# One meeting between phases, pads written by ScalarE, ternary weights prepared later, and products that nothing reads

## The reference

```
x = x + L0_xattn(layernorm(x), ctx)     # phase xatt0: q, wq, o, wp quantised to int8 steps, 16 heads of 16
x = x + L0_ffn(layernorm(x))            # phases gqa (causal attention) and moe0 (8 experts, top 2)
x = x + L1_xattn(layernorm(x), ctx, mask)   # phase mask_bit, first part
x = x + L1_ffn(layernorm(x))                # phase mask_bit, second part
x = x + L2_xattn(layernorm(x), ctx)     # phase xatt2
x = x + L2_ffn(layernorm(x))            # phase arrow
x = x + L3_xattn(layernorm(x), ctx)     # phases qkv3 and attend3
x = x + L3_ffn(layernorm(x))            # phase moe3

   # L1_xattn: one head of width 256, masked
scores = where(mask, x @ ctx.T / 16, -1e30);  out = softmax(scores) @ ctx
   # L1_ffn: three ternary weight matrices of 256 x 1024
weight_quant(w): s = 1 / max(mean(|w|), 1e-5);  clip(round(w * s), -1, 1) / s
gate, up = bit_linear(x, w_gate), bit_linear(x, w_up)
out = bit_linear(subln(up * relu(gate) ** 2), w_down)      # bit_linear also rounds x to 8-bit steps
   # L3_xattn: q, k rounded to 8-bit steps per row, v per column
q, k, v = qdq(x @ Wq / 4), qdq(ctx @ Wk), qdq(ctx @ Wv)
```

## Time and profile before

| | us |
|---|---|
| median of 3 runs | 3013.79 |
| lowest, highest | 3013.21, 3014.51 |
| the profiled execution | 3008.75 |
| its span | 3007.0 |

### The profile page before, as it was taken

How to read it: one execution, slowest core, us unless ns; L and a number is a source line. 1 busy time by engine, 2 the same in 40 slices (tenths; PEclk the granted TensorE clock), 3 DMA queues, 4 the chain that set the end, 5 groups by cost and what they waited for, 6 DMA issues and landing times. The chain is left out here.

```text
span 3007.0 us, 51047 instructions
## 1 busy us (share of the span) xinstructions
PE 2461.1 (82%) x19764; PEld 1665.5 (55%) x19788; DVE 2106.1 (70%) x4548; ACT 1633.5 (54%) x2824; POOL 543.0 (18%) x410
## 2 busy tenths in 40 slices
PE   6969999987999575897976577777777777779999
PEld 4736676764666343674655444444444444446666
DVE  7857878764352586775757799999999999942231
ACT  4534545543233364443434588888888888832222
POOL 2224333321221233221320400000000000012121
PEclk9989999998999677999998799999999999989999
DMA  3120000002000211101012300000000000000000
GB/s 136 39 78 6 11 8 18 6 4 77 21 22 11 91 36 67 33 26 43 29 43 89 133 9 9 15 9 9 14 17 9 9 15 9 3 27 21 11 11 11
DMA packets 58942, 92.83 MB, mean 31 GB/s; under 512 B 5440, under 2 KB 54608, under 8 KB 57680
## 3 DMA queue, kind: packets, MB, share of 16 engines
q1 hardware_dynamic: 58704, 89.57, 8.9%
HBM read 66.48 MB, written 23.07 MB: 30 GB/s over the span
## 5 line engine op out<-in xcount | busy, mean ns | idle before, releaser
L2595 ACT ACTIVATE attend_ex<-psum,attend_mx,queries_step 128x1024 uint16<-128x1024 f32 x512 | 618.0, 1207 | 122.0 <-DVE attend_mx L2626 122.0
L2697 PEld LDWEIGHTS psum<-ident_b,attend_ex 128*128 128x128 bf16 x4096 | 250.3, 100 | 398.9 <-issue 397.8
L2697 PE MATMUL psum<-ident_b,attend_ex 128*128 128x128 bf16 x4096 | 326.4, 225 | 157.0 <-DVE attend_pw L2630 125.9
L2685 PE MATMUL psum<-keys_turned,queries_ahead 96*128 96x512 bf16 x1024 | 320.1, 396 | 79.5 <-ACT attend_ex L2595 74.6
L1460 PE MATMUL psum<-arena,moe_tokT 128*128 128x512 f32 (+2 forms) x896 | 362.0, 549 | 3.3 <-DVE moe_h L1347 3.3
L2619 DVE TENSOR_REDUCE attend_mx<-psum 128x1 f32<-128x512 f32 x512 | 329.8, 686 | 26.1 <-PE psum L2685 7.8
L2615 DVE TENSOR_REDUCE attend_mx<-psum 128x1 f32<-128x1024 f32 x256 | 311.2, 1216 | 7.2 <-PE psum L2685 7.1
L1347 DVE TENSOR_TENSOR moe_h<-moe_sg,psum 128x512 f32<-128x512 f32 (+1 forms) x112 | 69.9, 625 | 267.0 <-PE psum L1460 257.5
L1460 PEld LDWEIGHTS psum<-arena,moe_tokT 128*128 128x128 f32 x896 | 166.5, 192 | 139.4 <-issue 120.9
L1194 ACT ACTIVATE moe_sg<-psum 128x512 f32<-128x512 f32 (+1 forms) x112 | 61.4, 548 | 287.1 <-PE psum L1460 282.8
L1130 POOL IOTA moe_index<- 128x8 f32 x2 | 0.3, 142 | 1007.0 <-POOLq L67 1007.0
(11 more groups left out here) (457 smaller groups left out, 4800.8 us busy)
## 6 DMA issues: line engine op xcount, KB each, us to landing
residual<-stored_rows SPq DMA_DIRECT2D x48, 128.0 KB, 1.7
queries_turned<-queries_rows SPq DMA_DIRECT2D x16, 384.0 KB, 3.1
queries_ahead<-queries_turned SPq DMA_DIRECT2D x16, 384.0 KB, 3.3
arena<-in_moe SPq DMA_DIRECT2D x1, 5704.0 KB, 16.4
arena<-in_gqa SPq DMA_DIRECT2D x1, 5440.0 KB, 18.4
arena<-in_moe SPq DMA_DIRECT2D x1, 4360.0 KB, 13.3
xatt_ct<-in_ctx_T SPq DMA_DIRECT2D x32, 128.0 KB, 2.3
residual<-stored_rows SPq DMA_DIRECT2D x16, 256.0 KB, 2.2
```

Of the source, the lines that this page charges most:

```text
L2595: nc.scalar.activation(ex[:, u % 4], S[:, u % 3], ACT.Exp, bias=mx[:, t % 2, h, 4:5], scale=steps[:, 0, t, h:h + 1], accum_out=sums[:, t % ...
L2685: last = nc.tensor.matmul(S[:, u % 3, b * 512:(b + 1) * 512], qt[:, t % 2, h * P:(h + 1) * P], KT[:, c:c + 4, h // 2], start=True, stop=True)
L2697: last = nc.tensor.transpose(TP[:, c], counts[u % 4][:, c * P:(c + 1) * P], k["ident_b"][:])
```

## The change

Six edits in one.

1. `end_phase` is gone. Between phases only the meeting at the end of the block is left. The semaphores of the last two phases are held, and the spent ones are cleared by POOL inside the next phase (`clear_spent`, at one place of each phase's POOL program). At the end of the program `end_program` has the two meetings and the clears.
2. The pads of xatt0 and xatt2 are written by ACT as 11 strided activations (Copy of `neg_half` broadcast, times a factor; together 2304 elements a partition), ahead of its other work; `Qp` in qkv3 as one activation of 128 x 3072.
3. gqa's causal mask is made behind the second `rstd`, and PE waits for it only before the first scores.
4. The ternary preparation in moe0 comes later: sums at steps 3 to 5, total at 6, steps, clamps and rounds at 6 and 7, casts at 7 to 9.
5. mask_bit: the mask is the first DMA, and x_norm of the first pair comes ahead of the wait for it.
6. `keep_busy`: products of `ident_b` with itself (128 x 512, bf16) that nothing reads, on PE: in mask_bit 12 at step 0 and 7 at each of steps 1 to 7, between `down` and `turn_b`; in qkv3 5 at the start of each of steps 1 to 16, from step 3 behind a wait for `qT`. 141 products in all.

```diff
-def end_phase(nc, sems):
-
-    numbers = sorted(s.num for s in sems.values())
+def semaphores(nc, k, phase, names):
+    if len(k["held"]) == 2:
+        k["held"].pop(0)[0].close()
+    stack = ExitStack()
+    sems = {n: stack.enter_context(nc.semaphore(phase + n)) for n in names.split()}
+    k["held"].append((stack, sorted(v.num for v in sems.values())))
+    return sems
+
+def clear_numbers(nc, numbers):
+    start = numbers[0]
+    for n, following in zip(numbers, numbers[1:] + [-1]):
+        if following != n + 1:
+            nc.gpsimd.sem_clear(range(start, n + 1))
+            start = following
+
+def clear_spent(nc, k):
+    if len(k["held"]) == 2:
+        clear_numbers(nc, k["held"][0][1])
+
+def end_program(nc, k):
     nc.all_engine_barrier()
-    nc.gpsimd.sem_clear(range(numbers[0], numbers[-1] + 1))
+    for _, numbers in k["held"][1:]:
+        clear_numbers(nc, numbers)
     nc.all_engine_barrier()
...
+def keep_busy(nc, k, bank, n):
+    for _ in range(n):
+        nc.tensor.matmul(k["psum"][:, bank, :], k["ident_b"][:], k["ident_b"][:].unsqueeze(1).to_broadcast([P, 4, P]), start=True, stop=True)
...
@@ xatt0 and xatt2, POOL @@
-            nc.gpsimd.memset(qkp[:], 0.0).then_inc(s["padded"], 1)
-            nc.gpsimd.memset(v[:], 0.0).then_inc(s["padded"], 1)
...
@@ xatt0 and xatt2, ACT @@
+            for r in range(3):
+                fill(qkp[:, r, 0:NH, HD:32], 0.0)
+                fill(qkp[:, r, NH:2 * NH, HD + 1:32], 0.0)
+                fill(qkp[:, r, NH:2 * NH, HD:HD + 1], 1.0)
+            fill(v[:].rearrange("p r h d -> p (r h) d")[:, :, HD + 1:32], 0.0)
+            fill(v[:].rearrange("p r h d -> p (r h) d")[:, :, HD:HD + 1], 1.0)
...
@@ gqa, POOL, in its loop; and PE, in scores @@
+                if i == -3:
+                    causal_mask()
+                    clear_spent(nc, k)
+                if t == 0 and 0 in banks:
+                    pe.wait_ge(s["mask_made"], 2)
...
@@ moe0 @@
-                if ternary and i == 4:
+                if ternary and i == 6:
                     weight_total()
-                if ternary and 1 <= i <= 3:
-                    weight_sum(i - 1)
+                if ternary and 3 <= i <= 5:
+                    weight_sum(i - 3)
-                if ternary and i == 5:
+                if ternary and i == 6:
                     weight_step()
...
@@ mask_bit @@
+            sp.dma_start(mi[:], masks[:, 0:1, :].rearrange("b o m -> o b m")).then_inc(s["m_loaded"], 16)
             load(0)
-            sp.dma_start(mi[:], masks[:, 0:1, :].rearrange("b o m -> o b m")).then_inc(s["m_loaded"], 16)
...
+            x_norm(0)
             dve.wait_ge(s["m_loaded"], 16)
             nc.vector.tensor_scalar(nm[:], mi[:], 1.0, -NEG, ALU.subtract, ALU.mult).then_inc(s["neg_mask"], 1)
-            x_norm(0)
...
                 at(down, i - 2)
+                if i == 0:
+                    keep_busy(nc, k, 0, 12)
+                elif i < NI:
+                    keep_busy(nc, k, 6, 7)
                 at(turn_b, i)
...
@@ qkv3 @@
             for i in range(-2, B + 1):
+                if 1 <= i <= B:
+                    if i >= 3:
+                        pe.wait_ge(s["qT"], 2 * i - 4)
+                    keep_busy(nc, k, 2 * ((i - 1) % 2), 5)
                 at(turn_k, i - 1)
```

More of the change, by code:

```diff
@@ L300, in _, with fill @@
         def _(act):
+            def fill(where, value):
+                like = k["neg_half"][:].unsqueeze(2).to_broadcast([P, where.shape[1], where.shape[2]])
+                nc.scalar.activation(where, like, ACT.Copy, scale=-2.0 * value).then_inc(s["padded"], 1)
+            for r in range(3):
[4 more added lines that the diff above has]
+            fill(v[:].rearrange("p r h d -> p (r h) d")[:, :, HD:HD + 1], 1.0)
             def turned_k(t):
@@ L739, in _, with causal_mask @@
         def _(pool):
[L740 to L743, removed]
+            def causal_mask():
+                nc.gpsimd.memset(cmask[:], 0.0).then_inc(s["mask_made"], 1)
+                pool.wait_ge(s["mask_made"], 1)
+                nc.gpsimd.affine_select(out=cmask[:], in_=cmask[:], compare_op=ALU.is_ge, fill=NEG, base=0,
+                                        pattern=[[0, 4], [-1, P]], channel_multiplier=1).then_inc(s["mask_made"], 1)
             def rstd(t):
@@ L1222, in _ @@
                     turned_src(i)
[L1223 to L1226 removed]
+                if ternary and 3 <= i <= 5:
+                    weight_sum(i - 3)
+                if ternary and 7 <= i <= 9:
+                    weight_cast(i - 7)
                 for j in range(PAIR):
@@ L1664, in _, with fill @@
                 at(keep, i + 6)
+                if i == -5:
+                    clear_spent(nc, k)
         @block.scalar
         def _(act):
+            def fill(where, value):
+                like = k["neg_half"][:].unsqueeze(2).to_broadcast([P, where.shape[1], where.shape[2]])
+                nc.scalar.activation(where, like, ACT.Copy, scale=-2.0 * value).then_inc(s["padded"], 1)
+            for r in range(3):
+                fill(qkp[:, r, 0:NH, HD:32], 0.0)
+                fill(qkp[:, r, NH:2 * NH, HD + 1:32], 0.0)
+                fill(qkp[:, r, NH:2 * NH, HD:HD + 1], 1.0)
+            fill(v[:].rearrange("p r h d -> p (r h) d")[:, :, HD + 1:32], 0.0)
+            fill(v[:].rearrange("p r h d -> p (r h) d")[:, :, HD:HD + 1], 1.0)
             def turned_k(t):
@@ L2313, in _ @@
         def _(pool):
-            nc.gpsimd.memset(Qp[:], 0.0).then_inc(s["padded"], 1)
             def rstd(t):
@@ L2585, in _ @@
             finish_next(sp, s["weights_next"])
+        @block.gpsimd
+        def _(pool):
+            clear_spent(nc, k)
         @block.scalar
```

60 lines of the change are left out of this document (26 added, 34 removed).

## The result

| | before, us | changed, us |
|---|---|---|
| median (4 runs each) | 3013.5 | 2986.43 |
| lowest, highest | 3013.08, 3014.51 | 2982.61, 2992.34 |
| the profiled execution | 3008.75 | 2982.61 |
| its span | 3007.0 | 2980.8 |

The ratio is 0.9911, with a 95% interval of 0.9895 to 0.9926: 27 us faster. The forecast was 2980, with a range of 2963 to 2998. The time is inside the range, and the total gain is four fifths of the forecast. The changed kernel's runs lie 10 us apart, those of before 1.4 (in later rounds before ranged over 3005.5 to 3017.3 too).

A forecast was written before the change was run, and what follows sets the result against it. Nine phases run one after another, each with its own limit, and TensorE's clock is held back in mask-bit and qkv. Terms of 33.8 us off 3008.75, plus 5.04 to the median, gave 2980 us, range 2963 to 2998.

The forecast's parts named there:

- Single meetings: At the eight inner phase boundaries, one meeting goes and POOL's clears cost nothing: -9.1 us (between -8 and -10).
- Pads: ACT's fills replace POOL's memsets, so the starts come earlier: xatt2 -3.0, qkv -1.6, xatt0 -1.2 us.
- Causal mask: In gqa, an operation slowed beside POOL's affine select (0.67 against 0.22) gets its time back: -0.45 us.
- Ternary: In moe0, waits at step 1 go (-5.0 us), and a new wait for POOL's total comes (+4.2): net -0.8.
- then it ran at half clock, of which 1.7 is loss: In moe0, PE's 3.40 us at half clock behind its 3.33 us wait; the 1.7 loss counted within the -5.0.
- The fall behind the new wait: In moe0, PE's clock falls after waiting for the ternary total: 1.7 us at two in three, counted as 1.2.
- Start of mask-bit: Norming x ahead of the wait for the mask makes x ready at 987.8 and not 990.4: -2.65 us.
- The products: Products that nothing reads hold PE's clock in some steps: mask-bit -8.4 us (0 to -20), qkv -6.6 (0 to -11.6).
- The small terms: All terms of the forecast other than the products' clock gains in mask-bit and qkv: 18.8 us in sum.
- the one in which the clock doesn't move: Rival for mask-bit and qkv: the products leave the clock unmoved, only 18.8 us gained, 2995 us; chance 0.20.
- the one in which it holds: Rival: the clock holds nearly everywhere, mask-bit gains 19.6 and qkv 11.6, 50.0 us in all, 2964 us; chance 0.20.
- The products stood in nobody's way: Answers the slower rival: exposed products push the work behind them, 3063 us if wholly exposed; chance 0.03.

The follow-up runs named there:

- the two other profiles above: The changed kernel with the pads written by POOL as before, 2994.12 us, and the changed kernel with the ternary total a step earlier, 2981.8 us.

## Why the prediction was right

**Single meetings** (-9.1): the gaps gave 9.7, right. That POOL's clears cost nothing fits their rows. What I did not have is that phases of unchanged code change their length with the meetings, arrow and moe3 in every such kernel; 6.8 arrived when done alone.

**Pads** (-3.0, -1.6, -1.2): xatt2 3.3, qkv 1.4 by its first copy; both right in mechanism and size. xatt0's start is quicker (the first product of PE at 11.07 in place of 13.15, ACT's first work on the weights at 12.00 in place of 13.27), but its length differs by more than that from one execution to the next, so the 1.2 is not shown in the phase.

**Causal mask** (-0.45): the operation took 0.22, and gqa is 0.5 shorter. gqa spans 522.0 to 524.5 over kernels with the same code, so the phase proves nothing.

**Ternary** (-5.0 and +4.2): the wait of ACT is gone and the new wait on POOL is there at 2.96 and 3.19, as worked out. But the 1.7 for the clock in the first term was not this edit's: moe0 kept its full clock with the old steps too, once the meetings were single (271.97 us with these alone). The net of the edit was +0.4, not -0.8. The step that failed is "then it ran at half clock, of which 1.7 is loss" as part of what goes. The fall behind the new wait, to which I gave two in three, came in one of the eight profiles with the total at step 6 (that with POOL's pads, moe0 274.46 us long).

**Start of mask-bit** (-2.65): 2.65 by PE's first turn.

**The products** (-8.4 and -6.6): the two terms failed in opposite ways in the profile of the changed kernel. Mask-bit gave 0.1 in place of 8.4. Two things were mis-sized there. A held step is worth 2.0 (by the run with fourteen products), not 2.8; DVE is busy 16.9 of its 18.4 us. And 1.96 us of idle time were enough for the fall each time in that profile, where I had one in three holding (in the two other profiles above it was three of seven); with 0.4 left it held at that place. I had also counted the first step as filled; 3.2 of its 6.6 us were left idle, since part of the twelve ran at full clock. qkv gave 10.7, where I had 6.6: the clock held through seven steps on end, and so behind three idle pieces of 2.6 to 2.9 us, which I had at one in four. In the seven other profiles with five products each it gave 5 to 7.5 (137.6 to 140.2 against 145.1), so the forecast 6.6 is nearer to those, and the changed kernel's own profile is at the good end. The Trainium skill (TensorE: Matmul & The Clock Gate, HAM oscillation) describes a rate that falls in each wait of a loop and is won back behind it; the windows of qkv without the products agree, at 0.82 on average, and with five a step the falls stop for the first seven steps.

**What was missing:** arrow +2.1, moe3 +1.2 and attend3 +1.1, 4.4 in sum. The last may be nothing, since attend3 took 936.3 to 938.7 in the other kernels with the same code. The small terms were right in sum: without the products the gaps, xatt2, mask-bit, qkv and moe0 gave 18.9 in the profile, against 18.8, and the median moved by 16.5. The products together gave 10.8 against 15.0, and that is luck in part: one term came out at nothing, and the other above its size in one good profile.

The rivals: neither of the two on the clock came out as put. Mask-bit in the changed kernel's profile followed the one in which the clock doesn't move, and the first half of qkv the one in which it holds. The products stood in nobody's way: in no profile was mask-bit or qkv longer with them than in the profiles without, even at 19 a step.

## What to carry to other kernels

Work that keeps PE's clock up pays only if what bounds the step is PE: read from DVE's busy time in a step what a held clock can give at most, and do this before counting products. Cheap tests decide how many are needed, since less than 2 us of idle time left was at times enough for a fall and at times not. POOL's all-reduce needs its 5.6 to 6.0 us ahead and 7 behind in a stretch where nobody waits for POOL; moving it one step earlier was worth 3 us. And when a profile differs from another by a few us, compare phases with unchanged code first: they show what the measurement does by itself.

## What the runs showed of the hardware

- The same code, xatt0, took 173.4 to 178.8 us in ten kernels, and gqa 522.0 to 524.5, with a granted clock in xatt0 of 0.985 in the shortest and 0.949 in the longest. Such differences can make the 10 us between the changed kernel's runs; no run isolates it.
- PE has idle pieces of 1.5 to 2.1 us in every second step of arrow. One of them led to a fall of the clock in mid-phase, at the same step in all ten kernels with single meetings and no products in arrow, and none did in the two with the old meetings; with seven products in them, there was none in the middle of the phase in two kernels. The piece ahead of the fall lasts 1.98 to 2.13 us in the ten and 1.81 in the two. Why the fall comes at this step and not another stays open.
- Mask-bit's steps of 20.4 us were two stretches of 10.2 at the two levels, step after step, with no drift. My reading, which no run isolates, is that step and clock had locked to each other. With 14 products the stretch at half clock was 6.8 us long in four steps, and then it was absent for 68 us.
- POOL's clears of semaphores take 46 to 399 ns each inside the phases of the changed kernel (14 of them, at most two a phase), and 281 to 673 between the meetings of the kernel before (nine, median 611).
- POOL sat idle 5.6 to 6.0 us ahead of its all-reduce and 7.0 to 7.3 us behind it in the three kernels where it was read, while no engine held it.
